# The same pieces of work in another written order on four engines of a fused two-layer kernel

## What is computed

```python
# layer 0
xn = layernorm(x)
x = x + linear_attention(xn) + moe(xn)
#   attention: q, k, v of 16 heads x 64, q and k l2-normalised along the sequence,
#     softmax(8 * q k^T) over 64 x 64 per head, times v, times w_out
#   moe: scores = sigmoid(xn @ gate_w.T) over 64 experts, best 4 of 8 groups, best 8 experts,
#     rw = weights of the chosen experts, 0 elsewhere (a dense 2048 x 64 table)
expert_out = vmap(lambda gw, uw, dw: silu(xn @ gw.T) * (xn @ uw.T) @ dw.T)(Wg, Wu, Wd)
moe_out = einsum('eth,te->th', expert_out, rw) + shared_mlp(xn)
# layer 1
xn = layernorm(x)
x = x + window_attention(xn) + bitlinear_ffn(xn)
#   window attention: 8 heads x 16; distances of each token to the 64 before it,
#     dist = sqrt((diff * diff * m_h).sum(-1) + 1e-8), top-32 of them, exp(-d) normalised,
#     weighted sum of values, a small linear map, a gate, then the decoder
#   ffn: ternary weights, squared ReLU, hidden 512, plus a rank-16 path
```

## Time and profile before

| | us |
|---|---|
| median of 3 runs (680.79 to 680.95) | 680.8 |
| the profiled execution | 682.07 |
| its span | 680.3 |
| TensorE busy | 642.2 |
| TensorE weight loads (beside the matmuls) | 435.5 |
| VectorE busy | 550.7 |
| ScalarE busy | 444.3 |
| GpSimd busy | 367.6 |

### The profile page before, as it was taken

The page is one execution under the profiler, slowest core; times in us unless marked ns, Lnnn a source line. Parts: engine busy times, 40 slices in busy tenths (PEclk is TensorE's granted clock), DMA queues, the critical chain, the costliest instruction groups (busy, mean ns, idle before and its releaser), DMA issues.

```text
span 680.3 us, 14252 instructions
## 1 busy us (share of the span) xinstructions
PE 642.2 (94%) x4792; PEld 435.5 (64%) x4792; DVE 550.7 (81%) x2461; ACT 444.3 (65%) x802; POOL 367.6 (54%) x448
## 2 busy tenths in 40 slices
PE   4888999999999999999999999999999999998785
PEld 3555765667556666766666567666657766675674
DVE  5998688746967999997986999984477999937996
ACT  3675454646687868557688877446879855478762
POOL 2288366646363688755463895665653577511220
PEclk9999899999999899999999999999999999999898
DMA  8930000000000000000000000000000000000000
GB/s 299 402 116 1 0 1 0 1 0 1 0 1 1 2 2 1 1 1 1 2 0 2 2 2 1 1 1 1 1 1 2 2 1 1 1 17 2 18 17 17
DMA packets 12968, 15.81 MB, mean 23 GB/s; under 512 B 1728, under 2 KB 10832, under 8 KB 12384
## 3 DMA queue, kind: packets, MB, share of 16 engines
q1 hardware_dynamic: 12896, 14.91, 6.3%
HBM read 13.85 MB, written 1.05 MB: 22 GB/s over the span
## 4 chain that ended last, share of the span: by engine, by line
PE 70%; DVE 18%; ACT 5%; POOL 3%; issue 3%; DMA 0%; DVEq 0%; POOLq 0%; ACTq 0%
PE bank_A L523 19%; PE bank_G L523 16%; PE bank_U L523 16%; PE bank_X L523 16%; DVE Wk L1269 4%; DVE m L1266 3%; DVE S L850 2%; DVE GWk L850 2%; PE bank_X L816 1%; PE bank_X L532 1%; ACT Ed L1336 1%; ACT L1341 1%; POOL PR L1643 1%; POOL Wlo L1643 1%; ACT L1336 1%
## 5 line engine op out<-in xcount | busy, mean ns | idle before, releaser
L1643 POOL TENSOR_TENSOR Wlo<-Wgu,Whi 128x256 fp32r<-128x256 f32 x184 | 136.2, 747 | 135.1 <-ACT Whi L1336 134.3
L523 PE MATMUL bank_A<-S,WdT 128*128 128x512 f32 x346 | 171.4, 598 | 0.2 <-POOL S L1643 0.2
L850 DVE TENSOR_TENSOR S<-S,bank_U 128x512 f32<-128x512 f32 x173 | 116.6, 682 | 35.1 <-PE bank_U L523 21.3
L1643 POOL TENSOR_TENSOR S<-S,Rb 128x512 f32<-128x512 f32 x84 | 109.3, 1302 | 56.4 <-DVE S L850 55.9
L523 PE MATMUL bank_G<-xH,Whi 128*128 128x512 f32 x184 | 99.6, 541 | 4.5 <-POOL Wlo L1643 2.3
L1336 ACT ACTIVATE Whi<-Wgu 128x256 fp32r<-128x256 f32 x184 | 73.4, 412 | 40.8 <-PE bank_U L523 36.1
L523 PE MATMUL bank_U<-xH,Whi 128*128 128x512 f32 x184 | 96.7, 525 | 0.1
L523 PEld LDWEIGHTS bank_A<-S,WdT 128*128 128x128 f32 x346 | 62.7, 190 | 33.9 <-issue 23.3
L1269 DVE MATCH_REPLACE8 Wk<-m,Wk 128x79 f32<-128x79 f32 x384 | 82.1, 225 | 0.0
L1336 ACT ACTIVATE S<-bank_G 128x512 f32<-128x512 f32 x90 | 53.6, 596 | 43.1 <-PE bank_G L523 37.9
L850 DVE TENSOR_TENSOR S<-Rb,bank_G 128x512 f32<-128x512 f32 x83 | 56.3, 679 | 25.6 <-ACT bank_G L1336 20.0
(11 more groups left out here) (294 smaller groups left out, 1184.9 us busy)
## 6 DMA issues: line engine op xcount, KB each, us to landing
Wgu<-in_Wgu SPq DMA_DIRECT2D x2, 2048.0 KB, 14.2
xs<-in_x SPq DMA_DIRECT2D x4, 256.0 KB, 6.0
wqk<-in_w_qkv SPq DMA_DIRECT2D x1, 1024.0 KB, 7.2
Wgu<-in_Wgu SPq DMA_DIRECT2D x1, 1024.0 KB, 8.9
out<-xs SPq DMA_DIRECT2D x3, 256.0 KB, 2.3
Wgu<-in_Wgu SPq DMA_DIRECT2D x1, 512.0 KB, 5.1
wout<-in_w_out SPq DMA_DIRECT2D x1, 512.0 KB, 7.7
wvT<-in_wvT SPq DMA_DIRECT2D x1, 512.0 KB, 8.5
```

Of the source, the lines that this page charges most:

```text
L523: return engine.matmul(dst, lhsT, rhs, start=start, stop=stop)
L850: return engine.tensor_tensor(dst, a, b, op)
L1643: return engine.tensor_tensor(dst, a, b, op)
```

## The change

Only four strings of `ORDER` differ: those of TensorE, VectorE, ScalarE and GpSimd. SyncE's is the same. Each new string holds every letter as often as the old one; the functions that the letters call are untouched, and so are all tiles, buffers and semaphores. The two orders hold the same number of table loads (38 named L1336, 35 at L1341, one at L1510). One line of each kind from the diff:

```diff
     "dve":
-        "yyycyyyyyyyyyeycyyyyyyyeayyyayyyyyyeecyyyyeeyyameemamaemeeamaeuuaumeeumeuuuuueaumeaemeeyymeeyyyyyyme"
+        "yyycyyyyyyyyyeycyyyyyyeayyyayyyyyyeecyyyyeeyamyeemamaemeemaaeuuaumeuemeuuauuuuemeaemeyeymeeyyyyyyym"
...
     "act":
-        "yxxyxyeexexcexcxeayaxeyxxesesxeaexsexsxexeaxexaeaexuxexueexxuuuyeyexxeexxexeexxeexexxeexxyexeyxeexxs"
+        "yxxyxyeexexcexxecayaxesyxxseexesaexesxxxeeaxexaeaexxuxeeuxeuuyuxyexeexxeexxxeexexexexexexyexseeyxees"
...
```

More of the change, by code:

```diff
@@ L44 @@
     "pe":
[L45 to L53, removed]
-    "dve":
-        "yyycyyyyyyyyyeycyyyyyyyeayyyayyyyyyeecyyyyeeyyameemamaemeeamaeuuaumeeumeuuuuueaumeaemeeyymeeyyyyyyme"
[L56 to L61, removed]
+        "yeyeyeeemeeaeaemaayeeaseeeseeameesmaeesemmmemmeeeemeemumaeeaeeaumeeeueaueemyeeymmmymeeeeemmeeemmeeee"
@@ new lines @@
+        "mmeeeemeeemeeeemyemesmeeseememeemsmeemeeeemeemeeeemmsemeeeememeemeeeemyemeymmeemeeeehymeeeemmmemeeme"
+        "mheehheehehemehhemmyeemeehmmmeheheeeaeeadeademdeeemeaemmdeadeematmeeteadmeedememmtedteeeemeetmmeeete"
+        "mtmmeteemmeetemmmeeeemteaeeetmmtameaeeeteetememameemmseeeeesmeeseeetseeemhtmytmeeetymmtemhteheyeeemh"
+        "memheheememmehheeemyehemhmheaeeaeeeemdeedaedeemeadeammdaedateeeteemmmmedemmeetmmeeetdeeeemmeateamema"
+        "eeemmteeteaeeemmesmtestmesemteeeetmestmmeeeememeeeemmeeeetemeamthmmteeeeeamtheatmaehtaeeeteatemmhame"
@@ new lines @@
+        "emehheemhheeeememehmehmehaeeemeedeadeedmememamdeamdeeetfemtdefeemmdeemmfeteetdemeeeeeemteememeetmete"
+        "mmetmeetmeeeetmmeeetemtmeeetmetemeeemeeetetmmtmmmthvvtfvhfhhvvhhtfvhhfvhhhdfvfddvdvdttddtdfvtvffvfvv"
+        "ttfvttfvfvtvtttvtttttttttt",
+    "dve":
+        "yyycyyyyyyyyyyeycyyyyyyeayyyayyyyyyeecyyyyeeyamyeemamaemeemaaeuuaumeuemeuuauuuuemeaemeyeymeeyyyyyyym"
+        "eeyyyyyymeeyyymeyeyymeemeyyyyemeeyymeemeemeemeemeemeeeemeeyymeehhyyyymheyyeyyyhhmeeymyeyyhyeyyyyymeh"
+        "hehhmeyehmehehahmaehemekkkemkkkkakekekakkmekkekkmgekeamagekmaeekkgkmkegekkemekekmkagekkgemekkekkgkmk"
+        "keeakmeekmkgeayeyyekemeeygymeehghhmehhgyyyemgyyyyyeyyyyyyyhemeyeyyymyeyhhhemhehyhaemeehmeahemhekkkkk"
+        "kakaemeakkegkkmeekmekkakkakemeekagkmeekkmgekkkkkmeeakkeakgmeekkgmekgkkemeekkkkmeekmeekgeemeaghhghehh"
+        "ameemgeaemgeahgaemeaaemehhhehahmehemehehmheekkakmekkakkemkkegkkmeekkkekkkmeekmegkekmkegkekmkekgkekme"
+        "gekkmegekkkmegkmekkeekgmekemgeekkkghhhhhghghhhhhhhhhkkkkkkkkkkkkkkgkkkkkkkkkgkkkkkkkkkkggkkkkkkgkkgk"
@@ L69 @@
-        "xkekfexxennegxfxxenexexexenexxexgenxegexxeexxegexxegxexeexeegmgfhfhhhoffhhhfhohhhhkfnnkfkknnnnkkfnnf"
-        "gnnknnkfgfnnfnnffqfgfgfgqgfgqggq",
+        "yxxyxyeexexcexxecayaxesyxxseexesaexesxxxeeaxexaeaexxuxeeuxeuuyuxyexeexxeexxxeexexexexexexyexseeyxees"
+        "xxxsexeexxxeexexexexexexesxeyxxemeyexexxxexehxeexhehhexxohohxeheehhxyexxexhexhhkkeexknxknenkaeexnaxk"
+        "nnxkenxgexeakxnneexxngexeexxexexngnexegxexeaxxexeexegaaxxegxeexexexesxxseexesymesegxxxyexhygexhexhox"
+        "eoehxehxexhheehhxeyxxhhehxekxekexnkexnnankaxxnnxkenekkageexxkxenenxgeexxneaxxeexaenaneexxgexxexesxgs"
@@ L71 @@
+        "esxeexxgexexexexexesxeexxmgehxeexxghaeaxgeexxhaehxeooxhhexehaxehheexhxxhhexakkeenkxxnenanekxxknneken"
+        "kgfxxkexfenxnexgenexxexeexxexnexgneegxexxeexxeegxxeegxxexeeegmgfhfhhhoffhhhfohhhhhkfnnfkkknnknngnnnn"
+        "kknkffnnngffnfnffgfqgffgqgfgqggq",
     "pool":
-        "lyllllllalllmmmlaaacaclalamlllmalmlmlllmlyymllmlllmllmlmllymllmllmllmlllmllmlmlllmllmlylylmlllmllmll"
-        "hmllymlmllmhllmlllmlmlaqllmqallaamqllamlapmllaqllmlmlqlmpalllmlqlmlmlqllmlpmlllqlmllpmyylllmhlmllmyl"
@@ L74 @@
-        "mlhllmllmlllaqllaammlaqmllmalaqlalmlmallpqmllqlmllmplmqllmllmlqlmlplmqllllmllpmllalmhaalmlmaalalamhl"
-        "allmllmlmlqllmlqlmlqlmllmlplqmllmlmqlllmpllmqllmlqmlplmmqphhhqqqqqqqq",
+        "llylllllalmmlllmaaaclacalamlllmalmllmllmyylmlllmllmllmllmlymlllmmllmlllmlllmllmllmllmlylylmlllmllmll"
+        "mhllmlymhlllmllmlmllmlaqllmqallaamqllamplalamlqllmlmlmqlplalmllqmlqlmllmlpmllqllmllmylylplmlhllmlmly"
+        "mhllllmmllllaqllaammlaqmlmlalaqlalmlapmllqmlqlmllmllqmplllmlqmllmlmllqllpmlllmlamplhlaaamallaalmlmha"
@@ L76 @@
+        "lllmlmllmllqmlllqlmlqmllmlplmqlllmqmlllpmllqmllmlqlmplmmqphhhqqqqqqqq",
 }
```

## The result

The changed kernel takes **683.03 us** (median of 22 runs, 681.27 to 685.83) against 680.96 us for the kernel before in the same jobs (22 runs, 678.94 to 683.27). The ratio is 1.0033 with a 95% interval of 1.0023 to 1.0042: about 2.2 us **slower**, clear of the 0.2% that a measurement here can tell. The ratios in this document differ from those of the two medians by up to 0.0009, here 1.0033 against 1.0030, so a difference of two times is uncertain by 0.6 us from that alone. One execution of 1268 us (of an experiment) and one of 1024 us (of the kernel before) are left out of all medians and ratios. The forecast was 680.0 us and no measurable change. The time lies inside the range of 677.0 to 683.5, but on the side that had a chance of 0.28, and not by the mechanism that was named for it.

A forecast was written before the change was run, and what follows sets the result against it. TensorE was taken to bound the middle, dependent steps the start, VectorE's top-32 rounds the end. Terms +0.3 + 0.2 - 1.6 + 0 + 0.3 = -0.8 us from 680.8 gave 680.0 us, no measurable change; range 677.0 to 683.5.

The forecast's parts named there:

- The bound and the three regimes: Start a chain of dependent steps, middle TensorE's own work, last 57 us VectorE's top-32 rounds of fixed length.
- the 57 that I gave as the test: 57 us from the last batch's first MAX8 to the end; a shorter last stage would mean wrong altogether.
- first 60 us: Wait before the k-norm matmul goes, but is given back at g12: +0.3 us, bounds -1.6 and +1.0.
- routing weights: Batch 1: VectorE's sums come earlier but GpSimd starts no sooner: +0.2 us, bounds -1.0 and +1.0.
- y.0: Transpose of batch 0's normalised tile: nearly its whole 1.63 us wait goes, -1.6 us, bounds -1.63 and 0.
- y.2: Transpose of batch 2, 7.3 us earlier, finds its tile ready: 0 us, bounds 0 and +2.0 or +3.6.
- hand-over: Start of the last stage: turn2.7 before mo.3 and a later decode delay VectorE's rounds +0.3 us, bounds 0 and +1.3.
- other moves in the saturated middle I cost at nothing: Remaining moved pieces in the middle cost 0, covered by TensorE's work; without cover one late piece costs about 1 us.
- rival 2: Transpose of batch 2 comes too soon and TensorE waits 2.0 to 3.6 us: 682.5 us, chance 0.26.
- turn2.7: At the hand-over it stands before mo.3, moving mo.3 from 596.37 to about 597.5; most is absorbed.
- Rival 1, the clock: One half-clock stretch fewer in the middle, 1.7 us each: 678.3 us, chance 0.27.
- a sign of being wrong altogether: TensorE's busy time changing by over 2 us, which only the clock or mix of shapes could do.

The follow-up runs named there:

- p4_end: Order of before, with the changed order only from 590 us to the end on all four engines; 683.02 us, ratio 1.0026.
- p4_turn: Order of before with the changed order from 590 us on, but turn2.6 on TensorE two down projections later than there; 680.78 us, ratio 0.9991.
- p1_head: Order of before, with the changed order only in the first 60 us on all four engines; 682.85 us, ratio 1.0024.
- a_endold: The changed kernel with the order of before from 590 us on; 683.67 us, ratio 1.0034.
- h_pap: Order of before, with the changed order in the first 60 us on TensorE, ScalarE and GpSimd, VectorE's as before; 684.44 us, ratio 1.0063.
- l1a: Order of before, with the changed order only from 392 to about 442 us on all four engines; 685.06 us, ratio 1.0071.
- a_swap: The changed kernel with ScalarE's k-norm logarithm of batch 0 again in front of the third spread copy; 682.54 us, ratio 1.0032.
- l1b: Order of before, with the changed order only from about 442 to 590 us; 684.28 us, ratio 1.0060.

## Why the prediction was wrong

*The bound and the three regimes: right.* No gap in the top-32 rounds: from the first MAX8 to the end it was 57.08 us before and 56.7 to 57.2 in ten of the twelve experiments' profiles (57.44 and 56.12 in the others). In the changed kernel's it was 58.01, over the 57 that I gave as the test: a half-clock stretch at 669 us lay on the last transposes and what follows them, and VectorE waited 0.33 and 0.76 us there.

The terms against the traces, each part's kernel compared with that before at the first MAX8 of the last batch, counted from the `Gs` matmuls and with the half-clock stretches up to 590 us evened out at 1.6 and 1.2 us (an estimate from the profiles of equal lists). The hand-over is counted from u183:

| term | forecast | by the traces |
|---|---|---|
| first 60 us | +0.3 | +0.7 |
| 60 to 392 us (routing weights +0.2, y.0 -1.6) | -1.4 | -1.2 |
| 392 to 590 us (y.2 and all other moves) | 0 | +2.1 |
| hand-over | +0.3 | -0.6 with the changed late part, +1.4 with the old one |
| a half-clock stretch that goes with the head's wait | no term | up to 1.6 |

*The step that failed: "other moves in the saturated middle I cost at nothing".* From 392 to 590 us they cost 2.1 us in the trace and 1.9 us (by the ratio 1.2) in time; 1.7 of it stand in six waits of 0.15 to 0.44 us, five of them for a product of VectorE. There TensorE had no idle time at all before, so any wait is a loss; I had even written that nothing can be given back there, and then held "covered by TensorE's own work" to mean free. It means the opposite for a piece of TensorE that comes before its input or before its bank is free.

*First 60 us: too low, and the clock left out.* Forecast +0.3 with +1.0 as the upper bound; by its order the head costs 0.7 us, inside the bounds. The 1.01 us before the k-norm went, and g12 waited instead (forecast 2 us, measured 2.59); the 1.08 us at u8, behind VectorE's late normalisation, I had not seen. What lies outside the bounds is the clock: a half-clock stretch stood at the end of g12's wait in all three profiles of this head. I had priced stretches in the middle alone, as chance, and none that comes with a wait.

```profile
43.64 0.50 PE L523 MATMUL bank_U<-xH,Whi 128*128 128x512 f32 x1 [1.08 <-DVE wT L850]
...
58.28 0.77 PE L523 MATMUL bank_G<-xH,Whi 128*128 128x512 f32 x1 [2.59 <-POOL Wlo L1643]
```

*Batch 1's routing weights:* forecast +0.2; the wait went (-1.0, my lower bound). But VectorE's sums now stand ahead of the product that frees g26's bank, and g26 waits 1.16 us where it waited 0.31. The sum of both was right, the picture only half.

*y.0: right in size and in both reasons.* The wait of 1.63 us is gone. In absolute time the tile is ready no earlier (178.32 against 178.11), but the changed kernel is 1.09 us late at A45. Counted from A45 the logarithm's table load comes after 12.71 us where it came after 13.63, the tile is ready 0.89 us earlier, and 0.75 us more of TensorE's work stand ahead of y.0: together the 1.63. The forecast had 0.6 and 0.86.

```profile
172.26 1.28 ACT L1341 ACT_TABLE_LOAD   x1
...
177.21 1.11 DVE L855 TENSOR_SCALAR mo<-xs,mv,ln 128x128 f32<-128x128 f32 x4
...
178.47 0.63 PE L532 MATMUL bank_X<-cst,mo 128*128 128x128 f32 x4
```

*y.2: right, and rival 2 wrong.* Distance from mo.2 8.08 us (forecast 8.6), tile ready 7.94 us after it (forecast 6.6 to 8.5), no wait:

```profile
457.39 0.66 PE L532 MATMUL bank_X<-cst,mo 128*128 128x128 f32 x4
...
460.62 1.28 ACT L1341 ACT_TABLE_LOAD   x1 [4.36 <-DVE mv L917]
461.92 0.30 ACT L1336 ACTIVATE ln<-mv,cst 128x4 f32<-128x4 f32 x1
...
464.21 1.12 DVE L855 TENSOR_SCALAR mo<-xs,mv,ln 128x128 f32<-128x128 f32 x4
...
465.47 0.63 PE L532 MATMUL bank_X<-cst,mo 128*128 128x128 f32 x4
```

Here too the activation starts 0.02 us after its table load ends (460.62 + 1.28 = 461.90). The drain of about 1380 ns that the Trainium skill (*ScalarE: Activation LUTs*, "What ACT_TABLE_LOAD costs") adds to a switch is not there; with it the tile would have been ready 1.2 us after y.2's start.

*The hand-over:* forecast +0.3. In the changed kernel the first MAX8 gains 0.49 us on the piece u183; in the old company it loses over 1 us. I priced turn2.7, whose row confirms it (0.28 us of wait), and passed over turn2.6, which I had seen move by four down projections. Nor did I ask when its bank is free.

*Rival 1, the clock:* the half-clock stretches are too loosely tied to the order for a forecast. Up to 590 us p4_end, p4_turn and the kernel before run the same lists, and their profiles have stretches at 73.6, 227.2 and 374.0; at 226.2; and at 73.9 and 227.5. That is 1.7 us more or less of TensorE's work each time, and may be part of why single runs of one kernel spread over 4 us. It does not explain the losses by order: they stand in shifts that stay the same at every later piece.

*Signs and sums.* TensorE's busy time rose by 4.7 us (642.2 to 646.9), where a change of more than 2 was a sign of being wrong altogether, through the clock or the mix of shapes. It is the clock at least in part: this profile has one half-clock stretch more before the last stage and two more in it, and they lengthen busy rows. The ends of the range were rounded: rival 1 with its terms gives 676.8 and rival 2 at its full price 683.6.

Together: by the traces +0.7, -1.2, +2.1 and -0.6 are +1.0 us; the whole changed kernel has +1.4 by the same count (the stretch at 372.3 us taken at 0.7). The head's stretch would add up to 1.6 us in executions that have none with the old head, which is enough for the 2.2 us measured; how often they have none is known from profiles alone (six of eight). By the medians the parts give +2.1, -0.9, +1.9 and -0.6, together +2.4, but each of these is uncertain by about 1 us, and the last is 0 by the ratios; so that they add up is not shown by the times.

## What to carry to other kernels

Judge a reorder first where the bound engine has no idle time: there no wait can be won, and small ones are lost nearly in full (1.7 of the 2.0 us above), so "it is saturated" is a reason to leave the order alone. Written orders of several engines fit each other: a part that wins in one company loses in another, so move few pieces, and for each that moves ahead ask when its input and its buffer are free, on the engine that frees it. The best result here came from keeping the one stretch that won and then putting right the two places where a product of VectorE held up a bank.

## What the runs showed of the hardware

**A long wait of TensorE was followed by a stretch at half clock.** In the three profiles with the whole changed head (the changed kernel, p1_head and a_endold) the granted clock fell to half within 0.3 us of the end of g12's wait of 2.6 us, for 3.4 us. It fell 0.2 us after the wait of 2.98 us in h_pap and 1.3 us after that of 3.00 us in l1a. It did not after 1.74 us (a_swap) and 2.25 us (l1b), nor after the second long wait of h_pap, 2.57 us. In the last stage the four profiles with the new end (the changed kernel, p4_end, p4_turn, a_swap) have one wait of 3.94 us that ends between 635 and 640 us; in all four the clock fell 1.0 to 3.2 us after its start and stayed at half for 6.8 us. The other ten have no wait over 1.7 us there; six of them have a stretch of 3.4 us near 640 us, four none. So nine of the ten waits of 2.57 us or more behind the first one of the kernel have a fall of the clock in them or within 1.4 us of their end; that the one brings the other was not tried by itself. The same window of p1_head and of a_swap:

```profile
57.00:65.00 8.00, 6.94 (x19) 4.37 (x20) 7.49 (x14) 4.99 (x7) 6.94 (x9) 0.79 0.00 0
```

```profile
57.00:65.00 8.00, 6.53 (x22) 3.35 (x24) 7.76 (x14) 4.99 (x7) 7.63 (x9) 1.00 0.00 1
```

A mean of 0.79 over 8 us is 3.4 us at 1.2 GHz and the rest at 2.4 GHz. So such a wait can cost its own length and up to 1.7 us more. For the head the sizes fit: counted from the `Gs` matmuls A15 comes after 56.26 to 56.32 us in the six profiles with the old head and no stretch before it, after 57.83 and 57.88 in the two with one (before and p4_end), and after 58.64 to 58.70 in the three with the new head. The Trainium skill (*TensorE: Matmul & The Clock Gate*, "HAM oscillation — how this bites in real kernels") says the same of waits for transfers: the engine starts cold behind them. Stretches also come where TensorE has not waited, near 227 us in 9 of the 14 profiles, among the many small matmuls of the q-norm and the distances. That these bring them on was not tried.

**Executions of equal lists keep equal distances once the first 29 us are over, but not in them.** Before the `Gs` matmuls eight profiles of one head differ by 0.73 us (28.54 to 29.27). From there to u13, 31 us on, they agree within 0.03 us, and p1_head keeps its shift of 1.22 to 1.27 us on before over 440 us.
